# Steady groups of a fused attention and feed-forward kernel: values of the first half in one run, the first query projection behind the keys, squares beside the values of the second half

## The reference

```
a, ang = amplitudes ** dt, frequencies * dt          # per token
xr = [c*x0 - s*x1, s*x0 + c*x1]                      # c, s = a*cos(ang), a*sin(ang)

q, k, v = split(xr @ W_qkv.T)                        # 16 heads of 16
k = layernorm(k)                                     # over the 16 of a head
S_t = gamma * S_(t-1) + v_t k_t^T                    # over 64 positions
y_t = S_t q_t
x1 = x + y @ W_o.T

scores = tanh(x1 @ W1 + b1) @ v                      # one score per position
pooled = softmax(mask(scores)) @ x1 / count          # mask by prompt type

xq   = fake_quant_int8(pooled)                       # scale by the maximum of all
h    = fake_quant_int8(silu(xq @ Wg.T) * (xq @ Wu.T))
out  = x1 + h @ Wd.T
```

## Time and profile before

| what | us |
|---|---|
| median of 3 runs | 285.33 |
| lowest and highest of these | 284.72, 285.52 |
| the profiled execution's own time | 285.58 |
| its span, first to last instruction | 283.9 |
| PE busy | 269.5 (95%) |
| DVE busy | 233.7 (82%) |
| ACT busy | 167.0 (59%) |
| POOL busy | 141.8 (50%) |
| granted TensorE clock over the span | 1.0 |

### The profile page before, as it was taken

The page is one execution under the profiler, slowest core; times in us unless marked ns, Lnnn a source line. Parts: engine busy times, 40 slices in busy tenths (PEclk is TensorE's granted clock), DMA queues, the critical chain, the costliest instruction groups (busy, mean ns, idle before and its releaser), DMA issues.

```text
span 283.9 us, 10688 instructions
## 1 busy us (share of the span) xinstructions
PE 269.5 (95%) x4692; PEld 195.4 (69%) x4699; DVE 233.7 (82%) x474; ACT 167.0 (59%) x275; POOL 141.8 (50%) x136
## 2 busy tenths in 40 slices
PE   5999899899999999999999999999999999998995
PEld 5878689588879878878878987986854334442331
DVE  7989978589699697875777865866888999999995
ACT  2891566365467553454346146143698999947991
POOL 6919487870890593395287042003002577850561
PEclk9999999999999999999999999999999999999999
DMA  6980505303500800800620220220006822000167
GB/s 185 311 262 2 150 5 189 113 2 107 196 3 19 281 5 2 295 8 2 207 95 5 76 77 5 69 83 5 3 2 217 300 74 76 0 1 0 59 252 284
DMA packets 19278, 28.58 MB, mean 101 GB/s; under 512 B 1888, under 2 KB 9632, under 8 KB 19232
## 3 DMA queue, kind: packets, MB, share of 16 engines
q1 hardware_dynamic: 19232, 27.90, 29.8%
HBM read 19.48 MB, written 8.42 MB: 98 GB/s over the span
## 4 chain that ended last, share of the span: by engine, by line
PE 59%; DVE 22%; ACT 8%; issue 5%; POOL 3%; DMA 1%; DVEq 0%; ACTq 0%
PE psum L807 15%; PE psum L848 6%; PE psum L870 5%; PE psum L832 4%; PE psum L1211 4%; PE psum L1230 3%; PE psum L912 3%; POOL arena L532 2%; PE psum L988 2%; ACT silu L770 2%; DVE arena L1606 2%; PE psum L891 2%; DVE h_max L1610 2%; PE psum L951 2%; PE psum L994 2%
## 5 line engine op out<-in xcount | busy, mean ns | idle before, releaser
L1398 DVE TENSOR_TENSOR arena<-psum,xq_mem 128x512 f32<-128x512 f32 x64 | 39.7, 684 | 9.1 <-PE psum L832 9.1
L475 POOL TENSOR_TENSOR xT_lo<-arena,xT 128x512 fp32r<-128x512 f32 x14 | 17.6, 1280 | 43.9 <-ACT xT L614 43.9
L1211 PE MATMUL psum<-xq_mem,guT 128*128 128x512 bf16 x149 | 33.4, 379 | 0.5 <-POOL xq_mem L520 0.3
L599 ACT ACTIVATE arena<-psum,pmask 128x512 f32<-128x512 f32 x32 | 20.3, 684 | 16.8 <-PE psum L995 16.8
L1211 PEld LDWEIGHTS psum<-xq_mem,guT 128*128 128x128 bf16 x152 | 14.5, 98 | 19.1 <-DVE arena L1606 1.0
L848 PEld LDWEIGHTS psum<-arena 64*32 64x32 f32 x2048 | 21.7, 105 | 8.2 <-issue 8.0
L848 PE MATMUL psum<-arena 64*32 64x64 f32 x2048 | 25.9, 225 | 1.4 <-issue 0.9
L614 ACT ACTIVATE xT<-arena 128x512 fp32r<-128x512 f32 x14 | 8.1, 624 | 31.6 <-PE psum L807 25.0
L752 ACT ACTIVATE silu<-psum,gu_x 128x1024 f32<-128x1024 f32 (+1 forms) x24 | 25.0, 1046 | 2.5 <-PE psum L1211 1.4
L1610 DVE TENSOR_REDUCE h_max<-arena 128x1 f32<-128x1024 f32 (+1 forms) x24 | 25.9, 1123 | 0.2
L1415 DVE TENSOR_TENSOR yT_lo<-psum,yT 128x256 fp32r<-128x256 f32 x32 | 12.0, 416 | 10.4 <-ACT yT L608 10.4
(11 more groups left out here) (247 smaller groups left out, 745.4 us busy)
## 6 DMA issues: line engine op xcount, KB each, us to landing
arena<-in_x SPq DMA_DIRECT2D x9, 512.0 KB, 4.0
x_dram<-arena SPq DMA_DIRECT2D x8, 512.0 KB, 3.7
pooled<-x_dram SPq DMA_DIRECT2D x8, 512.0 KB, 4.3
out<-pooled SPq DMA_DIRECT2D x15, 256.0 KB, 2.2
xin<-in_x_t SPq DMA_DIRECT2D x7, 512.0 KB, 4.9
cs_rows<-cs_dram SPq DMA_DIRECT2D x12, 256.0 KB, 5.5
pooled<-in_w_qkv_t SPq DMA_DIRECT2D x3, 256.0 KB, 4.4
pooled<-in_w_down SPq DMA_DIRECT2D x1, 704.0 KB, 7.5
```

The costliest lines, as they stand in the source:

```text
L475: pool.tensor_tensor(xT_lo[:, k, :], xrotT[:, k, :], xT[:, k, :].bitcast(F32), ALU.subtract).then_inc(xl_ok, 1)
L599: act.activation(qblk[:, c, odd, :], Q_BANK[c][:, :], ACT.Identity, scale=pmask[:, odd:odd + 1]).then_inc(q_ok, 1)
L1211: mm = pe.matmul(o[:, 512 * half:512 * half + 512], gT[i][:, c, v * P:v * P + P], xq[:, c, TB * n + 512 * half:TB * n + 512 * half + 512], ...
L1398: dve.tensor_tensor(dec[:, c, r, :, :], bank[S_BANK[r]].rearrange("q (n k) -> q n k", n=PP), two_heads, ALU.mult).then_inc(dec_done, 1)
```

## The change

In a steady group (2 to 6) PE now does both value pairs of the first half in one run, then both key blocks and, right behind them, the first query block, then the squares, then both pairs of the second half. ACT copies the first half of y before the key banks instead of behind them. Group 0 gets the same PE order from there on, and its `sums_copy` moves ahead of `gu_scales` on DVE. In group 1 the squares and the values of the second half come before the first query block, and both halves of y are copied before its first query copies. Nothing is added or taken away on any engine; the shapes and the sizes stay.

```
@@ ACT, loop over g
-                if g + 1 < G and g != 1:
-                    k_copies(g + 1, 0)
-                    if g:
-                        k_copies(g + 1, 1)
                 y_copy(g, 0)
                 if g + 1 < G:
-                    if g == 0:
+                    if g != 1:
+                        k_copies(g + 1, 0)
                         k_copies(g + 1, 1)
+                    if g == 1:
+                        y_copy(g, 1)
                     q_copies(g + 1, 0)
-                y_copy(g, 1)
+                if g != 1:
+                    y_copy(g, 1)
@@ PE, loop over g
                     values_pair(0, 0)
-                    if g == 0:
-                        values_pair(0, 1)
+                    values_pair(0, 1)
                     if g != 1:
...
                         project_whole(K_BANK, 1, 1, k_mm)
+                    if g == 1:
+                        squares(g + 1, 0)
+                        squares(g + 1, 1)
+                        values_pair(1, 0)
+                        values_pair(1, 1)
                     if g:
-                        values_pair(0, 1)
                         pe.wait_ge(s_sub, g)
                     else:
                         pe.wait_ge(w1o_ok, 1)
-                    squares(g + 1, 0)
-                    if g:
+                    project_whole(Q_BANK, 0, 0, q_mm)
+                    if g != 1:
+                        squares(g + 1, 0)
                         squares(g + 1, 1)
-                    project_whole(Q_BANK, 0, 0, q_mm)
-                    values_pair(1, 0)
-                    values_pair(1, 1)
-                    if g:
-                        sums_turn(g + 1)
-                    else:
-                        squares(1, 1)
+                        values_pair(1, 0)
+                        values_pair(1, 1)
+                    sums_turn(g + 1)
                     project_whole(Q_BANK, 0, 1, q_mm)
-                    if g == 0:
-                        sums_turn(1)
@@ DVE, loop over g
                     low_y(g, 0)
-                    if g:
-                        sums_copy(g + 1)
+                    sums_copy(g + 1)
...
                 low_y(g, 1)
-                if g == 0:
-                    sums_copy(1)
```

## The result

The changed kernel takes 290.31 us (median of 4 runs, 289.51 to 293.27), against 285.42 for the kernel before on the same chip (284.72 to 285.79). The ratio is 1.0183, with a 95% interval of 1.0137 to 1.0228: slower by 4.9 us, where 286.1 was predicted and the range ended at 287.7. The profiled execution of the changed kernel is the 293.27, its span 291.5.

What follows compares the result with a forecast made beforehand. PE was taken to bound groups 3 to 6, DVE groups 1 and 2. Merging (-1.56), old pauses (-0.92), new fetch pauses (+3.16) and groups 0 and 1 (+0.1, -0.05) gave 286.1 us, 8-in-10 range 283.4 to 287.7.

Steps and rivals of the forecast that it cites:

- What merging saves: PE, groups 3 to 6: grouping value pairs and projections saves 0.39 us a group, 1.56 in all.
- The waits on other engines: Group 3: ACT's square is ready 0.6 us before PE wants it, DVE's copy of the sums 0.5 before; no cost.
- The pauses: PE waiting for instruction blocks: new pauses of 0.96, 0.8, 0.7 and 0.7 us in groups 3 to 6, 3.16 together.
- The interval from one block start to the next: Time PE needs between starts of 256-instruction blocks: at least 3.2 to 3.8 us, taken as 3.5.
- Sum: Whole kernel: 285.58 - 1.56 - 0.92 + 3.16 + 0.1 - 0.05 = 286.31 for a profiled execution, 286.1 as median.
- the old ones: Existing pauses in the second half's values, 0.36 us in group 3 and 0.56 in group 4, counted as removed: 0.92.
- Groups 0 to 2: Group 0 saves 0.05 us, group 1 ends 0.1 later (0 to 0.5), group 2 is bound by DVE: 0.
- Rival A: Fetch doesn't bind, blocks come in time: 282.8 us, or 283.8 if the old pauses stay; chance 0.22.
- Rival B: Same fetch mechanism at its long end, group 3's pause 1.65 and the others longer: 288.0 us; chance 0.33.
- Rival C: Kind changes cost as much elsewhere and pauses stay as they are: 285.4 us; chance 0.08.
- my case: The main forecast, merging's saving outweighed by new fetch pauses: 286.1 us, range alone 285.0 to 287.0; chance 0.37.
- What would show it wrong: Signs in the profile after: 128-pair runs at 1.41 us throughout, or a wait for ACT at the squares or DVE at the turn.

Runs made afterwards that it cites:

- shift_before: The kernel before with 22 tiny matmuls (88 instructions) added at the kernel's start, where PE waits for its first data: 289.09 us.
- half_after: The changed kernel with half as many matmuls of twice the columns in every value step, the odd heads' part left out: 278.99 us.
- half_before: The kernel before with half as many matmuls of twice the columns in every value step, the odd heads' part left out: 280.74 us.
- squares_free: The changed kernel with the squares from group 3 on replaced by same-shape matmuls that wait for nothing, key layernorm left out there: 287.57 us, ratio 1.0068.
- late_squares: The changed kernel with the squares of groups 2 to 6 moved between the second half's two value pairs, nothing left out: 286.01 us.
- late_wait: late_squares with one more wait, for ACT's plain copy of the first key bank, ahead of the first query block in groups 2 to 6: 288.78 us.
- steady_only: The changed kernel with groups 0 and 1 in the order of the kernel before: 292.48 us.

## Why the prediction was wrong, point by point

**What merging saves: right.** The first values' run took 1.41 and the 18 projections 4.35 for 4.31. Group 6 of after less its pause is 23.10 - 0.74 = 22.36; before's order takes 22.72 there and 22.77 in other groups without a pause (shift_before): 0.36 to 0.41, for 0.39. With half as many value matmuls it is 0.30 a group where no pause stands (groups 5 and 6), and half_after gains 1.75 on half_before by the medians.

**The waits on other engines: the numbers right, the reading wrong.** This is the step that failed. It said that ACT's key copies are pushed by 0.3, that the square is there at 103.85, and that PE wants the squares at 104.5, "covered by 0.6". In after the square ended at 104.59, 5.11 behind the first values (5.08 predicted), and PE took the squares at 105.24, 5.76 behind them (5.72), without a gap: covered by 0.65. But only the engine was asked. The sequencer is ahead of it: behind the run of values come 18 matmuls with their loads that take 4.35 us, it reaches the squares' wait 3.3 to 4.3 us early, and stands there, for 1.95 to 2.81 us. Before, the wait for the squares came behind 12 such matmuls and a pair of values, and the record in groups 2 to 6 is 0.05. What is held back with the sequencer on PE is also the request for its next block, which this step did not count. Where a block start had just been crossed, in groups 4 and 5, that cost the second pauses, 2.70 us together. By the ratios the time falls by 3.3 us without the wait (squares_free) and by 4.6 with the squares later (late_squares), and rises by 3.3 when the wait is put back (late_wait).

**The pauses: the places right, the sum wrong.** The four that were named are all there, at the places named: the second half's run in group 3 (121 loads, for "near load 120"), the third key matmul in group 4, load 104 in group 5, load 78 in group 6. They measure 2.11, 0.52, 0.73 and 0.74, where 0.96, 0.8, 0.7 and 0.7 stood in the sum. The three short ones were near; group 3's was outside its range of 0.25 to 1.65. This is the second step that failed, and it is not the squares' wait, since squares_free has 1.50 there without it. The interval from one block start to the next held: about 3.6 behind 105.5. (Counted by 256 instructions, the two of the kernel before are 3.4 and 3.9.) But the prediction started it at 103.85, when ACT's second square is out, 5.08 behind the first values, and PE came to that block start, in the squares, only 6.0 behind them. With 0.9 more the pause comes to 1.9, for 2.11 measured. The term that is missing is the second pause in groups 4 and 5, of 1.84 and 0.86. Their size is in the figure of 3.5 us from one block start to the next that PE needs: in after it is 135.31 - 128.04 = 7.3 in group 4 and 160.47 - 153.71 = 6.8 in group 5, as the fetch starts 4.9 and 4.5 behind the crossing. I took the range of 3.2 to 3.8 from two places of a kernel in which the sequencer never stood long, and used it as if it were a fixed latency. From landing to going on it is as predicted, 1.4 (133.89 to 135.31) for 1.5.

**Sum.** Pauses of 6.80 stand where 3.16 were predicted: 2.70 more by the second pauses of groups 4 and 5, 1.15 more in group 3, 0.2 less in the rest. Less the old ones, 0.92, and less 1.56, that is 4.3 us, near the 4.9 by which the medians differ, and near the 4.2 of the two shortest runs.

**Groups 0 to 2.** Group 1 had its pause, 1.15 marked, at 59.53, and the scores still came 0.30 sooner than before, where 0.1 later was predicted (0 to 0.5): PE's waits of 0.95 for s_sub and 0.42 for DVE are gone, more than the pause cost. Group 2 was equal within 0.07. Group 0's 1.06 is of this execution.

**The rivals.** Rival A (fetch doesn't bind) is out: its sign was a run of 1.41 throughout. By the rule of the Trainium skill, "Runtime: NRT & Kernel Launch", Instruction fetch mechanics, crossing a block is mostly hidden; the trace of after disagrees, with 6.8 us in six pauses. Rival B (slower, the same mechanism at its long end, 288.0) had the right sign, but it lengthened group 3's pause by ACT's square and a slow packet, where squares_free shows that it is not ACT, and it was still 2.3 too low, since it too had no second pauses. Rival C is out by the runs of 1.41. The range ended at 287.7 because both my case and rival B sized the pauses with the same two intervals. That the sequencer waits longer than the engine was in neither.

**What would show it wrong** named "a wait for ACT at the squares". In the engine's rows there is none. It was in the sequencer's.

## To carry to other kernels

When an instruction that waits on another engine is moved, ask when the sequencer gets to it, not when the engine does: behind a few long matmuls it gets there early, and what it can't do meanwhile includes asking for its next block. Where small matmuls use up 256 instructions in 2 to 4 us, put the waits so that few long instructions stand ahead of them, or make the small ones fewer, which took nearly all of both costs away here (half_after). A saving of 0.4 us a group by grouping like instructions is real only if the denser run doesn't outrun the fetch.

## What the runs showed of the hardware that I had not expected

- A sequencer in a semaphore wait puts off the fetch of the next block: crossing to fetch in group 4 was 1.1 to 1.2 us without the wait (squares_free, late_squares), 3.8 and 4.9 with it (late_wait, after). A wait that begins 0.7 us behind the crossing didn't (group 6, fetch 1.1 behind); one that began 0.4 behind did (group 5).
- 88 instructions more ahead of the kernel's first data cost 3.6 us (shift_before); the pauses of its groups 3 and 4 went, and new ones came in groups 0 and 1.
- 22 tiny matmuls in one column group took 1.48 us, 34 ns for each of the 44; spread over four column groups 0.47, 11 ns each.
- Behind pauses of 1.7 to 2.2 us the granted clock was at its lower level for a while, which makes a mean of 0.66 to 0.87 over stretches of 4 to 10 us (after, steady_only), and in other places a pause as long left it at 1.00. In after it is about 3.0 us of the 7.6 by which the profiled executions differ.
